# Expert outputs of a graph network's mixture layer: from VectorE multiply-adds to ScalarE scaling and TensorE sums in PSUM

## The chip, the cores and the metric

The kernel runs on one core of a Trainium2 chip. The metric is the device time of one execution in microseconds. The core has five engines with queues of their own: TensorE (PE in the rows; PEld its weight loads), VectorE (DVE), ScalarE (ACT), GpSimd (POOL) and SyncE (SP, which here only issues DMAs). They meet through semaphores.

## What is computed

Two layers on 32 graphs of 256 nodes with 128 features (8192 nodes, 64 tiles of 128). The first is a graph network (adjacency times features, two matrix products with RMS norm and SiLU). The second is a mixture of four experts whose gates come from graph attention over 524288 edges. Cut to what matters here:

```python
agg    = segment_softmax_sum(h[src], scores(src, dst), dst)     # graph attention, 4 heads x 4 experts
scores = layernorm(agg + b_gat).reshape(M, 4, 4).mean(heads)
topk_s, topk_i = top_k(scores, 2);  w = softmax(topk_s)
for e in range(4):
    g   = where(topk_i == e, w, 0).sum(-1)
    out = out + g[..., None] * (gelu(x @ W1[e] + b1[e]) @ W2[e] + b2[e])
return x + out
```

The expert outputs do not depend on the gates and are made long before them. What is late is the gates, and with them the last line's weighted sum of four expert outputs per node.

## The kernel before

The program is one launch with a hand-written order per engine. The stages, by the profile's time: sorting of the edges (to about 150 us), the graph network in a pipeline over 32 graphs (to about 460 us), the experts (to about 736 us), counting of edges (to about 905 us), and the **parts' stage**, from about 905 us to the end, which is all that the change touches.

The expert outputs (`eo`) of 64 tiles, 4 x 128 columns each, are ready when that stage begins. Those of the first 48 tiles lie in DRAM (`outputs`) in 12 blocks of 4 tiles; the last 16 tiles are kept in SBUF (`eo_kept`). GpSimd's 384 indirect gathers (L552), begun during the counting, fetch the table rows of the edges' sources, 96 per part. The stage does four **parts** g = 0 to 3 of 16 tiles each. A part is a chain over three engines:

- `hots_of` (L1400, VectorE) builds one-hot matrices; the copy of the gathered rows by heads (L948, ScalarE) is turned by TensorE (L782); `weights` (L1413, VectorE) does the softmax scans and ends in `back_ready`.
- TensorE turns the weights back (L787), ScalarE copies (L940), VectorE multiplies (`values`, L1437) and both split the rows into three bf16 pieces (`hi`, `remainder`, `mid`, `lowest`: L930, L1444, L935, L1449).
- TensorE sums them by owner in two batches of 48 matmuls (L795), into all eight PSUM banks: `sums[0]` is `ps_H`, `sums[1]` is `ps_four`, four banks each, four tiles of 3 x 24 columns to a bank. `take_bank` (L1451) reduces them; each raises `agg_out`.
- ScalarE issues a DMA that moves the odd half (L961); `merge` (L1461) waits for it; `gating` (L1501, about 40 small VectorE instructions) ends in `gates_ready`. In between, TensorE and ScalarE prepare the next part's marks (L771, L922 to L925).

**The weighted sum** stands between these steps. `combine(b)` (L1544, instruction L1557) is, for the block b of 4 tiles, 16 VectorE multiply-adds of 128 x 128 that read one expert's output, the gate column and the row of `xs`, and write `xs`. Part g does the four blocks of part g - 1: two while TensorE does the one-hot matmuls and two between `take_bank` and `merge`; the last part does two before `weights`, one and one. The blocks come back from DRAM through four SBUF slots (`SLOT_OF`, `load`, L453); a slot is free when its last block is combined, and SP stores each finished block (L485). After the last part's gates, VectorE does 8 kept tiles (32 multiply-adds), and the other 8 (`others`) go through ScalarE (scaling by the gates, L974) and GpSimd (three adds per tile, L590 to L594).

Of the kernel before, what the change touches and what calls it, by code (L numbers as in the profile page):

```python
# [24 lines left out]
GRAPHS, NODES, D = 32, 256, 128  # L25
# [39 lines left out]
PART_BLOCKS = BLOCKS // (PARTS - 1)  # L65
SLOT_OF = (0, 1, 0, 1, 0, 1, 2, 0, 1, 2, 3, 0)
KEPT_BLOCKS = 2

def build(nc, x, adj, eps, W1, b1, rms_w, W2, b2, W_gat, att_src, att_dst, b_gat, ln_g, ln_b,  # L70
# [4 lines left out]
    with ctx:  # L75
# [44 lines left out]
        def region(at):  # L120

            def take(shape, dt=fp32):
# [9 lines left out]
                if len(shape) > 1:  # L132
# [173 lines left out]
        sums = [ps_H[:, :, :, :].rearrange("p a b n -> p (a b n)").rearrange("p (g w) -> p g w", g=4), ps_four[:, :, :]]  # L306
# [17 lines left out]
                 "combined", "others_combined", "sum_chain", "gated", "iota_done", "zero_done"]  # L324
# [61 lines left out]

        def part_tiles(m, g):

            return m[:, g * PART_TILES:(g + 1) * PART_TILES]

        others = [(eo_kept[:, t, :], TILES - PAIR * KEPT + t) for t in range(KEPT_BLOCKS * BLOCK_TILES, PAIR * KEPT)]

# [3 lines left out]
        def _(sp):  # L396
# [100 lines left out]
            for b in range(KEPT_BLOCKS):  # L497
                sp.wait_ge(s["combined"], BLOCKS + b + 1)
                rstore(GROUPS - KEPT + BLOCK * b, BLOCK, out_stored[1])
            for b in range(KEPT // BLOCK - KEPT_BLOCKS):  # L500
                sp.wait_ge(s["others_combined"], BLOCK_TILES * (b + 1))
                rstore(GROUPS - KEPT + BLOCK * (KEPT_BLOCKS + b), BLOCK, out_stored[0])
            sp.wait_ge(out_stored[0], 16 * (KEPT // BLOCK - KEPT_BLOCKS))
            sp.wait_ge(out_stored[1], 16 * (BLOCKS + KEPT_BLOCKS))
# [5 lines left out]
        def _(pool):  # L510
# [73 lines left out]

            pool.wait_ge(s["gates_ready"], PARTS)
            for n, (of, t) in enumerate(others):
                row = xs[:, t, :]
                pool.wait_ge(s["gated"], n + 1)
                pool.tensor_tensor(of[:, 0:2 * D], of[:, 0:2 * D], of[:, 2 * D:4 * D], ALU.add).then_inc(s["sum_chain"], 1)  # L590
                pool.wait_ge(s["sum_chain"], 2 * n + 1)
                pool.tensor_tensor(of[:, 0:D], of[:, 0:D], of[:, D:2 * D], ALU.add).then_inc(s["sum_chain"], 1)
                pool.wait_ge(s["sum_chain"], 2 * n + 2)
                pool.tensor_tensor(row, row, of[:, 0:D], ALU.add).then_inc(s["others_combined"], 1)  # L594

        @block.tensor
        def _(pe):
# [178 lines left out]
            for g in range(PARTS):  # L776
                if g:
                    pe.wait_ge(s["agg_out"], 2 * g)
# [833 lines left out]
```

## Time and profile before

| | us |
|---|---|
| median of 3 runs (range) | 1173.28 (1170.89 to 1177.06) |
| profiled execution, whole time | 1177.35 |
| its span, first to last instruction | 1175.6 |
| parts' stage, from about 905 to the end of the span | about 270 |
| VectorE busy in the span | 918.5 (78%) |
| TensorE / ScalarE / GpSimd busy | 790.5 / 440.6 / 613.2 |

The profile is one execution. Times in its rows are from the start of the span. In a timeline row stand start, duration, engine, line, operation, output and inputs with their shape and the number of instructions merged (xN), and in brackets how long the engine had been idle and what released it.
### The profile page before, as it was taken

How to read it: one execution, taken by the hardware profiler on the slowest of the kernel's cores; microseconds unless marked ns; L12 is line 12 of the kernel's file. 1: busy time of each engine (PE TensorE's matmuls, PEld its weight loads, DVE VectorE, ACT ScalarE, POOL GpSimd, SP SyncE). 2: the span in 40 equal slices, each digit the busy share in tenths (PEclk: the TensorE clock that was granted, in tenths of full speed). 3: DMA queues.
4: the chain of work that ended last, by engine and by line, in shares of the span. 5: the costliest groups of instructions: out<-in, count | busy, mean ns of one | idle time of the engine just before them, and what ended most of it. 6: DMA issues, size and time to landing. Idle time of an engine off the chain costs nothing. (4 is left out here: it accounts for less than half of the span.)

```text
span 1175.6 us, 17882 instructions
## 1 busy us (share of the span) xinstructions
PE 790.5 (67%) x5180; PEld 677.8 (58%) x5180; DVE 918.5 (78%) x3070; ACT 440.6 (37%) x1069; POOL 613.2 (52%) x553
## 2 busy tenths in 40 slices
PE   0000089999999997987999999999997424131130
PEld 0000078887888885866888888888885314031030
DVE  7999967776888876999799800788887568888877
ACT  1009378775554553543555555000001212120203
POOL 2000000002777764057777777888888778888004
PEclk9999988997999996998999999655555555555555
DMA  7000011111222212121222221000000122616001
GB/s 248 0 0 1 7 42 38 44 43 45 48 53 56 56 9 12 54 78 46 64 81 81 63 63 10 7 7 7 7 6 9 10 48 51 182 29 203 19 22 36
DMA packets 73039, 55.42 MB, mean 47 GB/s; under 512 B 32534, under 2 KB 65689, under 8 KB 72988
## 3 DMA queue, kind: packets, MB, share of 16 engines
q1 hardware_dynamic: 56140, 48.72, 13.1%
q0 software_dynamic: 16384, 5.54, 5.7%
q10 hardware_dynamic: 464, 0.59, 0.2%
q8 instruction: 19, 0.31, 0.1%
q14 instruction: 32, 0.26, 0.1%
HBM read 36.65 MB, written 17.76 MB: 46 GB/s over the span
## 5 line engine op out<-in xcount | busy, mean ns | idle before, releaser
L552 POOL DMA_INDIRECT sb_arena<-table,sb_arena x384 | 465.1, 1211 | 169.7 <-issue 116.8
L536 POOL DMA_INDIRECT sb_late<-lists,sb_window_at x128 | 128.0, 1000 | 320.5 <-ACT sb_window_at L862 278.7
L727 PE MATMUL ps_four<-sb_late 128*128 128x64 bf16 x1232 | 160.3, 301 | 3.2 <-DVE sb_late L1287 0.9
L1285 DVE TENSOR_TENSOR sb_late<-sb_far_lo,sb_iota_lo 128x1792 bf16<-128x1792 bf16 x88 | 96.1, 1092 | 83.9 <-PE ps_four L727 81.7
L727 PEld LDWEIGHTS ps_four<-sb_late 128*128 128x128 bf16 x1232 | 141.9, 143 | 21.5 <-DVE sb_late L1287 19.6
L700 PE MATMUL ps_four<-sb_we,sb_arena 128*128 128x128 f32 x1024 | 131.9, 282 | 0.0
L700 PEld LDWEIGHTS ps_four<-sb_we,sb_arena 128*128 128x128 f32 x1024 | 119.7, 192 | 14.7 <-issue 14.7
L692 PE MATMUL ps_H<-sb_x2nT,sb_we 128*128 (+1 forms) x512 | 124.6, 388 | 0.0
L634 PE MATMUL ps_four<-sb_arena 128*128 128x256 f32 x128 | 38.8, 432 | 122.2 <-DVE sb_var L1145 122.2
L885 ACT ACTIVATE sb_arena<-ps_H,sb_be_c 128x256 f32<-128x256 f32 x256 | 107.2, 471 | 30.6 <-PE ps_H L692 28.7
L634 PEld LDWEIGHTS ps_four<-sb_arena 128*128 128x128 f32 x128 | 28.3, 227 | 129.4 <-DVE sb_arena L1198 122.5
L692 PEld LDWEIGHTS ps_H<-sb_x2nT,sb_we 128*128 128x128 f32 x512 | 95.1, 196 | 11.0
L818 ACT ACTIVATE sb_arena<-sb_arena,sb_owner_mid 128x368 f32<-128x368 f32 x128 | 76.8, 600 | 53.4 <-DVE sb_arena L1046 49.8
L626 PE MATMUL ps_H<-sb_arena,sb_w 128*128 128x256 f32 x256 | 78.5, 460 | 0.2 <-DVE sb_arena L1209 0.2
L1209 DVE SCALAR_TENSOR_TENSOR sb_arena<-ps_H,sb_b_c,sb_arena 128x256 f32<-128x256 f32 x128 | 53.1, 477 | 20.8 <-ACT sb_arena L844 19.6
L645 PE MATMUL ps_four<-sb_w,sb_arena 128*128 128x128 f32 x512 | 69.0, 290 | 0.0
L855 ACT ACTIVATE sb_arena<-sb_arena,sb_rms_c 128x256 f32<-128x256 f32 x128 | 54.6, 497 | 37.5 <-DVE sb_arena L1209 37.5
L669 PEld LDWEIGHTS ps_four<-sb_ones,sb_arena 128*128 128x128 f32 x512 | 60.8, 195 | 10.8 <-ACT sb_arena L834 10.8
L669 PE MATMUL ps_four<-sb_ones,sb_arena 128*128 128x1 f32 x512 | 60.7, 248 | 9.1 <-ACT sb_arena L839 9.1
L922 ACT ACT_TABLE_LOAD x1 | 1.3, 1283 | 170.6 <-PE ps_H L771 170.6
L645 PEld LDWEIGHTS ps_four<-sb_w,sb_arena 128*128 128x128 f32 x512 | 62.8, 200 | 3.9 <-issue 0.2
L782 PE MATMUL ps_H<-sb_ident,sb_iota_lo 128*128 128x128 f32 x24 | 7.1, 435 | 80.5 <-ACT sb_iota_lo L948 80.1
(244 smaller groups left out, 1466.4 us busy)
## 6 DMA issues: line engine op xcount, KB each, us to landing
outputs<-sb_arena SPq DMA_DIRECT2D x24, 512.0 KB
sb_arena<-outputs SPq DMA_DIRECT2D x12, 1024.0 KB, 6.7
sb_arena<-in_adj SPq DMA_DIRECT2D x32, 256.0 KB
sb_arena<-table,sb_arena POOLq DMA_INDIRECT x384, 2.9
sb_x2nT<-in_L_ffn_edge_index SPq DMA_DIRECT2D x8, 512.0 KB, 7.6
sb_xs<-in_x SPq DMA_DIRECT2D x32, 128.0 KB, 2.5
out_x<-sb_xs SPq DMA_DIRECT2D x16, 256.0 KB, 2.6
sb_late<-lists,sb_window_at POOLq DMA_INDIRECT x128
```

The source lines that it names most:

```text
L536: pool.indirect_dma_start(bk.bitcast(i32)[:, p * WINDOW:(p + 1) * WINDOW], None, lists, bass.IndirectOffsetOnAxis(ap=window_at[:, p:p + 1] ...
L552: pool.indirect_dma_start(rows[:, g, c, o, :], None, table[0:M, :], bass.IndirectOffsetOnAxis(ap=idxT[:, at:at + 1], axis=0), bounds_check ...
L626: last = nc.tensor.matmul(ps_H[:, q, c, :], w1[:, c * P:(c + 1) * P], aggT[:, q, :], start=True, stop=True)
L634: last = nc.tensor.matmul(ps_A, xn[:, p, mt, :], adjT[:, p, mt, :], start=(mt == 0), stop=(mt == 1))
L645: last = nc.tensor.matmul(ps_O[:, nt, :], ss[:, q, c, nt * P:(nt + 1) * P], w2[:, c, :], start=False, stop=(nt == 1 and c == HC - 1))
L669: last = nc.tensor.matmul(ps_Q[:, u:u + 1], sq[:, q, c, u * P:(u + 1) * P], ones[:, 0:1], start=(c == 0), stop=(c == HC - 1))
L692: last = nc.tensor.matmul(halfH[e][:, c * GROUP:(c + 1) * GROUP], we1[:, e, c * P:(c + 1) * P], x2nT[:, bass.ds(g * GROUP, GROUP)], start= ...
L700: last = nc.tensor.matmul(obank[k][:, (j // 2) * D:(j // 2 + 1) * D], hh[1 - p][:, j, k * P:(k + 1) * P], we2[:, j, :], start=False, stop= ...
L727: last = nc.tensor.matmul(ps_F, hot_lo[k][:, :, c], hot_hi[k][:, :, c], start=(first and c == 0), stop=(end and c == FB - 1))
L818: nc.scalar.activation(sign_out, owner, ACT.Sign, bias=owner_mid[:, o:o + 1], scale=2.0, accum_out=above[:, o:o + 1]).then_inc(s["above_co ...
L885: last = nc.scalar.activation(hh[p][:, 2 * e + c, :], halfH[e][:, c * GROUP:(c + 1) * GROUP], ACT.Gelu, bias=be1_c[:, 2 * e + c:2 * e + c ...
L1285: V.tensor_tensor(hot_lo[k], far_lo[:, bass.ds(b * FB, FB)].unsqueeze(1).to_broadcast([P, P, FB]), iota_lo[:, :, :], ALU.is_equal)
```

## The change

For the 12 blocks of the first three parts, VectorE's 16 multiply-adds per block are replaced by three steps on three engines: ScalarE scales the block's 16 pieces of 128 x 128 by their gates in place in the slot (`scale_block`), TensorE adds the four experts with four fp32 matmuls of 512 columns against the identity (`block_sum`), and VectorE adds the resulting bank to four tiles of `xs` in one instruction (`combine`). The banks for it come from packing six tiles instead of four to a bank in the one-hot sums (three banks per batch). Kept tiles: VectorE does ten, in groups of 4, 4 and 2; six go through ScalarE, TensorE (four experts and the row of `xs`) and ScalarE again; GpSimd's adds go. The stores of the kept tiles are of two tiles each.

```diff
+PER_BANK = 6
-KEPT_BLOCKS = 2
+KEPT_TILES = 10
...
+        sums = [ps_H[:, :, :, :].rearrange("p a b n -> p (a b n)").rearrange("p (g w) -> p g w", g=4)[:, 0:3, :], ps_four[:, 0:3, :]]
+        marks_bank = [halfH[2], bank_O[:, :]]
+        block_bank = [bank_S[:, :], halfH[3]]
...
+        def blocks_in(g):
+            if not g:
+                return [], []
+            of = [PART_BLOCKS * (g - 1) + b for b in range(PART_BLOCKS)]
+            return (of[:1], of[1:]) if g < PARTS - 1 else (of[:2], of[2:])
...
-            pool.wait_ge(s["gates_ready"], PARTS)
-            for n, (of, t) in enumerate(others):
...
             def mark(g):
                 if g:
-                    pe.wait_ge(s["agg_out"], 2 * g - 1)
+                    pe.wait_ge(s["agg_out"], 2 * g)
...
+            def block_sum(b):
+                pe.wait_ge(s["scaled"], b + 1)
+                some(pe, s["combined"], b - 1, None)
+                of = eo_back[SLOT_OF[b]]
+                for e in range(EXPERTS):
+                    last = nc.tensor.matmul(block_bank[b % 2], ident[:, :], of[:, :, e * D:(e + 1) * D],
+                                            start=(e == 0), stop=(e == EXPERTS - 1))
+                last.then_inc(s["block_in_psum"], 1)
...
                     last.then_inc(s["terms_in_psum"], 1)
+                for b in early:
+                    block_sum(b)
                 for k, ready in ((1, "back_ready"), (0, "exp_done")):
...
                 if g + 1 < PARTS:
                     mark(g + 1)
+                for b in late_:
+                    block_sum(b)
+            pe.wait_ge(s["agg_out"], 2 * PARTS)
+            for n, (of, t) in enumerate(others):
+                pe.wait_ge(s["gated"], n + 1)
+                for e in range(EXPERTS):
+                    nc.tensor.matmul(others_bank[n], ident[:, :], of[:, e * D:(e + 1) * D], start=(e == 0), stop=False)
+                nc.tensor.matmul(others_bank[n], ident[:, :], xs[:, t, :], start=False, stop=True).then_inc(s["others_in_psum"], 1)
...
+            def scale_block(b):
+                act.wait_ge(s["gates_ready"], b // PART_BLOCKS + 1)
+                act.wait_ge(eo_loaded[SLOT_OF[b]], 16 * turns(b))
+                for u in range(BLOCK_TILES):
+                    for e in range(EXPERTS):
+                        of = eo_back[SLOT_OF[b]][:, u, e * D:(e + 1) * D]
+                        last = nc.scalar.activation(of, of, ACT.Identity, scale=gates[:, b * BLOCK_TILES + u, e:e + 1])
+                last.then_inc(s["scaled"], 1)
...
+                if g < PARTS - 1:
+                    by_heads(g)
+                    for b in early:
+                        scale_block(b)
+                else:
+                    for b in early:
+                        scale_block(b)
+                    by_heads(g)
...
                 mid(2 * g + 1)
+                for b in late_[:2]:
+                    scale_block(b)
                 act.wait_ge(s["agg_out"], 2 * g + 2)
...
                 nc.scalar.activation(part_tiles(gates, g), part_tiles(sc, g), ACT.Exp).then_inc(s["gates_exp"], 1)
+                for b in late_[2:]:
+                    scale_block(b)
...
             def combine(b):
...
+                dve.wait_ge(s["block_in_psum"], b + 1)
+                to = xs[:, b * BLOCK_TILES:(b + 1) * BLOCK_TILES, :]
+                V.tensor_tensor(to, to, block_bank[b % 2].rearrange("p (t d) -> p t d", t=BLOCK_TILES), ALU.add).then_inc(s["combined"], 1)
...
                 take_bank(2 * g)
                 take_bank(2 * g + 1)
-                for b in before[len(before) // 2:]:
+                merge(g)
+                for b in late_[:1]:
                     combine(b)
-                merge(g)
                 gating(g)
-            for b in range(KEPT_BLOCKS):
-                combine(BLOCKS + b)
+                for b in late_[1:]:
+                    combine(b)
...
+            combine_kept(0, 4)
+            combine_kept(4, 4)
+            combine_kept(8, KEPT_TILES - 8)
```

So in the parts 1 and 2 one of the four blocks is early (`early`) and three are late (`late_`); in part 3 two and two. What is queued behind what is shown at two places. Line numbers in the rows of the change are those of the changed kernel.

VectorE from the end of part 2's gating to `weights` of part 3, before (L1541 ends the gating, L1404 is `hots_of`, L1557 the multiply-adds, L1418 the first instruction of `weights`):

```order
L1541 TENSOR_TENSOR sb_gates<-sb_gates,sb_gs 128x64
L1404 TENSOR_TENSOR sb_arena<-sb_arena,sb_w 128x1024 x6
L1557 SCALAR_TENSOR_TENSOR sb_xs<-sb_arena,sb_gates,sb_xs 128x128 x32
L1418 TENSOR_TENSOR sb_arena<-ps_H,sb_arena 128x384
L1420 TENSOR_TENSOR sb_arena<-ps_H,sb_arena 128x384
```

The same place in the change (L1605 ends the gating, L1612 is `combine`, L1467 `hots_of`, L1481 the first of `weights`):

```order
L1605 TENSOR_TENSOR sb_gates<-sb_gates,sb_gs 128x64
L1612 TENSOR_TENSOR sb_xs<-sb_xs,ps_four 128x512
L1612 TENSOR_TENSOR sb_xs<-sb_xs,ps_H 128x512
L1467 TENSOR_TENSOR sb_arena<-sb_arena,sb_w 128x1024 x6
L1612 TENSOR_TENSOR sb_xs<-sb_xs,ps_four 128x512
L1612 TENSOR_TENSOR sb_xs<-sb_xs,ps_H 128x512
L1481 TENSOR_TENSOR sb_arena<-ps_H,sb_arena 128x384
```

Blocks 6 and 7 now stand ahead of the one-hots, and 8 and 9 between these and `weights`; each is one instruction that waits for a bank.

ScalarE over the same stretch, before (L968 is the gates' exponential, L948 the copy by heads, L951 the softmax's exponential):

```order
L968 ACTIVATE sb_gates<-sb_sc 128x64
L948 ACTIVATE sb_iota_lo<-sb_arena 128x384 x2
L951 ACTIVATE sb_arena<-sb_arena 128x384
L940 ACTIVATE sb_arena<-ps_four 128x3x4x32 x2
L930 ACTIVATE sb_late<-sb_arena 128x48x24 x2
```

ScalarE there in the change (L1015, L981 and L996 are those three, L973 is `scale_block`):

```order
L1015 ACTIVATE sb_gates<-sb_sc 128x64
L973 ACTIVATE sb_arena<-sb_arena,sb_gates 128x128 x48
L981 ACTIVATE sb_iota_lo<-sb_arena 128x384 x2
L996 ACTIVATE sb_arena<-sb_arena 128x384
L963 ACTIVATE sb_arena<-ps_four 128x3x4x32 x2
```

The scaling of three blocks (7, 8 and 9), 48 instructions, now stands between the gates and the copy by heads.

TensorE in the change, from part 2's one-hot sums to those of part 3 (L809; L772 are the marks, L781 `block_sum`, L794 and L801 the two turns, which before followed each other directly as L782 and L787):

```order
L809 MATMUL ps_four<-sb_late,sb_arena 64x72 x48
L772 MATMUL ps_H<-sb_arena,sb_epsI 128x384
L772 MATMUL ps_four<-sb_arena,sb_epsI 128x384
L781 MATMUL ps_H<-sb_arena,sb_ident 128x512 x4
L781 MATMUL ps_four<-sb_arena,sb_ident 128x512 x4
L781 MATMUL ps_H<-sb_arena,sb_ident 128x512 x4
L794 MATMUL ps_H<-sb_ident,sb_iota_lo 128x128 x6
L781 MATMUL ps_four<-sb_arena,sb_ident 128x512 x4
L781 MATMUL ps_H<-sb_arena,sb_ident 128x512 x4
L801 MATMUL ps_four<-sb_ident,sb_arena 128x128 x6
```

The sums of the blocks 5, 6 and 7 stand ahead of the first turn, and those of 8 and 9 behind it.

## Rows read from the trace of the kernel before

**Rows 1.** The page: span, and the granted TensorE clock in 40 slices.
```profile
span 1175.6 us, 17882 instructions
...
PEclk9999988997999996998999999655555555555555
```

**Rows 2.** Timeline, part 1's last take_bank to weights of part 2.
```profile
999.55 1.41 DVE L1458 TENSOR_REDUCE sb_late<-ps_four 64x192 f32<-64x576 f32 x2 [0.89 <-PE ps_four L795]
...
1000.89 4.27 DVE L1557 SCALAR_TENSOR_TENSOR sb_xs<-sb_arena,sb_gates,sb_xs 128x128 f32<-128x128 f32 x16
...
1006.62 4.29 DVE L1557 SCALAR_TENSOR_TENSOR sb_xs<-sb_arena,sb_gates,sb_xs 128x128 f32<-128x128 f32 x16 [1.46 <-DMA sb_arena<-outputs]
...
1010.82 0.22 DVE L1467 TENSOR_TENSOR sb_a_dst<-sb_late,sb_far_e 128x64 f32<-128x64 f32 x1
...
1027.38 0.22 DVE L1541 TENSOR_TENSOR sb_gates<-sb_gates,sb_gs 128x64 f32<-128x64 f32 x1
1027.64 3.70 DVE L1404 TENSOR_TENSOR sb_arena<-sb_arena,sb_w 128x1024 bf16<-128x1024 bf16 x6
...
1031.26 0.55 DVE L1418 TENSOR_TENSOR sb_arena<-ps_H,sb_arena 128x384 f32<-128x384 f32 x1
```

**Rows 3.** Timeline, part 0: merge with no multiply-adds ahead of it, then gating.
```profile
949.30 0.23 DVE L1467 TENSOR_TENSOR sb_a_dst<-sb_late,sb_far_e 128x64 f32<-128x64 f32 x1 [4.87 <-DMA sb_late<-sb_late]
...
953.41 0.19 DVE L1505 TENSOR_SCALAR sb_late<-sb_late 128x64 f32<-128x64 f32 x1
...
964.77 0.26 ACT L968 ACTIVATE sb_gates<-sb_sc 128x64 f32<-128x64 f32 x1 [14.41 <-DVE sb_sc L1536]
...
965.86 0.22 DVE L1541 TENSOR_TENSOR sb_gates<-sb_gates,sb_gs 128x64 f32<-128x64 f32 x1
```

**Rows 4.** Timeline, part 2's last take_bank to weights of part 3.
```profile
1061.07 1.41 DVE L1458 TENSOR_REDUCE sb_late<-ps_four 64x192 f32<-64x576 f32 x2 [0.88 <-PE ps_four L795]
...
1063.95 7.94 POOL L552 DMA_INDIRECT sb_arena<-table,sb_arena  x1 [0.31 <-issue]
...
1091.23 8.48 DVE L1557 SCALAR_TENSOR_TENSOR sb_xs<-sb_arena,sb_gates,sb_xs 128x128 f32<-128x128 f32 x32
1092.69 2.21 ACT L948 ACTIVATE sb_iota_lo<-sb_arena 128x384 f32<-128x384 f32 x2 [6.16 <-DMA sb_arena<-table,sb_arena]
...
1093.99 1.86 PE L782 MATMUL ps_H<-sb_ident,sb_iota_lo 128*128 128x128 f32 x6 [30.10 <-ACT sb_iota_lo L948]
...
1099.63 0.55 DVE L1418 TENSOR_TENSOR sb_arena<-ps_H,sb_arena 128x384 f32<-128x384 f32 x1
```

**Rows 5.** Timeline, part 3's last take_bank to the end of the multiply-adds.
```profile
1129.44 1.41 DVE L1458 TENSOR_REDUCE sb_late<-ps_four 64x192 f32<-64x576 f32 x2 [4.35 <-PE ps_four L795]
1130.78 4.27 DVE L1557 SCALAR_TENSOR_TENSOR sb_xs<-sb_arena,sb_gates,sb_xs 128x128 f32<-128x128 f32 x16
...
1151.57 9.46 ACT L974 ACTIVATE sb_x2nT<-sb_x2nT,sb_gates 128x128 f32<-128x128 f32 x32 [1.09 <-DVE sb_gates L1541]
1151.58 16.54 DVE L1557 SCALAR_TENSOR_TENSOR sb_xs<-sb_x2nT,sb_gates,sb_xs 128x128 f32<-128x128 f32 x32
```

**Rows 6.** Timeline of TensorE: fp32 passes of 256, 128 and 384 columns.
```profile
725.60 2.05 PE L700 MATMUL ps_four<-sb_we,sb_arena 128*128 128x128 f32 x16
727.49 1.89 PE L692 MATMUL ps_H<-sb_x2nT,sb_we 128*128 x8
...
942.91 2.93 PE L771 MATMUL ps_H<-sb_arena,sb_epsI 128*128 128x384 f32 x4
```

**Rows 7.** Windows (PE, PEld, DVE, ACT, POOL busy; clock; DMA): experts' start, and counting.
```profile
462.00:464.00 2.00, 2.00 (x6) 1.55 (x6) 0.13 (x2) 0.28 (x1) 0.00 (x0) 0.50 0.11 16
...
466.00:468.00 2.00, 2.00 (x11) 1.74 (x11) 1.93 (x4) 1.99 (x6) 0.00 (x0) 1.00 1.39 39
...
750.00:800.00 50.00, 48.14 (x378) 43.16 (x377) 43.88 (x55) 0.00 (x0) 41.77 (x28) 0.50 0.07 7
```

**Rows 8.** The page's DMA issues: size and time to landing.
```profile
sb_arena<-outputs SPq DMA_DIRECT2D x12, 1024.0 KB, 6.7
```

More of the change, by code:

```diff
@@ L583, in _ @@
                     edge_tile(2 * j + 1, 1)
-            pool.wait_ge(s["gates_ready"], PARTS)
-            for n, (of, t) in enumerate(others):
[L588 to L594, printed above, removed]
         @block.tensor
@@ L975, in _, with keep_sum @@
                 last.then_inc(s["gated"], 1)
+            def keep_sum(n):
+                act.wait_ge(s["others_in_psum"], n + 1)
+                nc.scalar.activation(xs[:, others[n][1], :], others_bank[n], ACT.Identity).then_inc(s["others_combined"], 1)
+            gate(0)
+            gate(1)
+            for n in range(2, len(others)):
+                gate(n)
+                keep_sum(n - 2)
+            keep_sum(len(others) - 2)
+            keep_sum(len(others) - 1)
         @block.vector
@@ L1453, in take_bank @@
                 dve.wait_ge(s["agg_in_psum"], k + 1)
[L1454 to L1458 removed]
+                for first, past, each in ((0, 2, PER_BANK), (2, 3, BATCH - 2 * PER_BANK)):
+                    by_bank = sums[k % 2][0:OWN, first:past, 0:each * 3 * ROW].rearrange("p g (t u s v) -> p g t u s v", u=2, s=3, v=ROW)
+                    at = BATCH // 2 * (k % 2) + first * PER_BANK // 2
+                    for u, m in enumerate((agg, odd)):
+                        o = m[k // 2 % 2][0:OWN, at:at + (past - first) * each // 2, :].rearrange("p (g t) v -> p g t v", g=past - first)
+                        last = V.reduce_sum(o, by_bank[:, :, :, u, :, :].rearrange("p g t s v -> p g t v s"), AX.X)
                 last.then_inc(s["agg_out"], 1)
@@ L1567, in _ @@
                 if g == PARTS - 1:
-                    combine(before.pop(0))
-                    combine(before.pop(0))
+                    for b in early:
+                        combine(b)
                 weights(g)
@@ L1575, in _, with combine_kept @@
                 lowest(2 * g + 1)
-                for b in before[:len(before) // 2]:
-                    combine(b)
+                if g < PARTS - 1:
+                    for b in early:
+                        combine(b)
                 take_bank(2 * g)
                 take_bank(2 * g + 1)
-                for b in before[len(before) // 2:]:
+                merge(g)
+                for b in late_[:1]:
                     combine(b)
-                merge(g)
                 gating(g)
-            for b in range(KEPT_BLOCKS):
-                combine(BLOCKS + b)
+                for b in late_[1:]:
+                    combine(b)
+            def combine_kept(first, n):
+                base = (EXPERTS - 1) * first
+                for e in range(EXPERTS):
+                    for u in range(n):
+                        row = xs[:, TILES - PAIR * KEPT + first + u, :]
+                        if e:
+                            dve.wait_ge(s["comb_chain"], base + (e - 1) * n + u + 1)
+                        last = V.scalar_tensor_tensor(row, eo_kept[:, first + u, e * D:(e + 1) * D],
+                                                      gates[:, TILES - PAIR * KEPT + first + u, e:e + 1], row, ALU.mult, ALU.add)
+                        if e < EXPERTS - 1:
+                            last.then_inc(s["comb_chain"], 1)
+                        elif u % PAIR:
+                            last.then_inc(s["combined"], 1)
+            combine_kept(0, 4)
+            combine_kept(4, 4)
+            combine_kept(8, KEPT_TILES - 8)
 _INS = ["x", "adj", "L0_gnn_epsilon", "L0_gnn_W1", "L0_gnn_b1", "L0_gnn_rms_weight", "L0_gnn_W2", "L0_gnn_b2",
```

69 lines of the change are left out of this document (27 added, 42 removed).

## The prediction, blind

> **What bounds the kernel now.** I read the page first, then the timelines of the three places where one part hands over to the next, and last the windows that show TensorE's clock. The page [rows 1] says that the span is 1175.6 us and that in its last 14 slices the granted clock is about half. Everything that the change touches lies in the last 270 us, so the prediction is a sum over a few boundaries there; the rest stays as it is.
>
> I write W(g) for the start of `weights` of part g. Two readings from the rows decide what a saved VectorE microsecond is worth.
>
> First, from W(2) at 1031.26 [rows 2] to the end of part 2's second `take_bank` at 1062.48 [rows 4] it is 31.2 us, and from W(3) at 1099.63 [rows 4] to 1130.85 [rows 5] it is 31.2 us again. By the kernel's order two blocks of multiply-adds stand inside the first stretch and one inside the second. A block is 4.27 us [rows 2], and yet the stretches are equal: TensorE's one-hot sums cover them. Taking multiply-adds out **there** is worth nothing.
>
> Second, between `take_bank` and `merge` they are seen: part 1 goes from 1000.96 to 1010.82 [rows 2] with two blocks and a wait of 1.46 for a load. But part 0 [rows 3], with no block there, has VectorE idle for 4.87 at the same place, for the DMA of the odd half. So about half of what is taken out here comes back as that wait.
>
> The next readings give the length of each boundary before. `take_bank` of part 1 to W(2): 1000.96 to 1031.26, 30.3 us [rows 2]. `take_bank` of part 2 to W(3): 1062.48 to 1099.63, 37.2 us [rows 4]; here the gathers are late too (the copy by heads waits 6.16 for them, until 1092.69), and the 8.48 of two blocks end last. `take_bank` of part 3 to the gates: 1130.85 to 1151.57, 20.7 us; then 16.54 of multiply-adds on the kept tiles [rows 5].
>
> **The change part by part: the price of a block.** ScalarE scales 16 pieces of 128 x 128. The same instruction on the kept tiles takes 9.46 for 32 [rows 5], 0.296 each: 4.7 us per block. VectorE's add of 512 columns from PSUM has no row; the nearest is 0.55 for 384 columns from PSUM [rows 2], so about 0.7.
>
> TensorE's four fp32 matmuls of 512 columns are eight passes. No row of before has such a block. From both sides: four passes of 384 columns at a clock of 0.50 take 2.93 [rows 6], so eight of 512 take 2.93 x 2 x 512/384 = **7.8**; eight passes of 256 columns at 1.00 take 1.89 [rows 6], so eight of 512 take **3.8**. Which clock is granted? In the counting stage TensorE is busy 48.14 of 50 us and has 0.50 throughout, with narrow bf16 matmuls; when the experts begin, with fp32 passes of 256 columns back to back, the window from 462 has 0.50 and that from 466 has 1.00 [rows 7]. The sums are like the second. I take the middle, **5.8**, for a block that comes after a pause and 3.8 for one directly behind another.
>
> The Trainium skill says it the same way for the second case and not for the first: its page "TensorE: Matmul & The Clock Gate" (Part 1, the HAM clock gate) has the throttled clock as the default, which sustained activity releases. By that rule the sums end at the high clock and the total below is about +17; by the row of the counting stage, where a busy engine was not released, it would be about +35. The experts' windows are why I lean to the first.
>
> **From `take_bank` of part 1 to W(2).** In the change: the wait for the odd half, 4.9; `merge`, 949.30 to 953.41, 4.1; block 1's add, 0.7 (its sum is ready after the marks' 2.9 and 5.8, that is at 8.7, when VectorE comes at 9.0); gating, 953.41 to 966.08, 12.7 [all rows 3]. That is 22.4 to the gates. Then block 3. ScalarE has it behind the gates' exponential, which ends 1.05 before the gates are done (965.03 against 966.08 [rows 3]). From there 4.7 to scale, 5.8 to sum, 0.7 to add: 10.2 after the gates. The one-hots (3.7 [rows 2]) are queued behind that add on VectorE, so W(2) comes at 22.4 + 10.2 + 3.7 = 36.3, against 30.3: **+6.0**.
>
> **From `take_bank` of part 2 to W(3).** Again 22.4 to the gates. ScalarE now has 48 scalings (blocks 7, 8, 9) ahead of the copy by heads, where before the copy was next. On the path: 14.2 for these, from 1.05 ahead of the gates; the copy, 2.2; TensorE's turn, which ends at 1095.85, 0.95 after the copy [rows 4]; only then the sums of 8 and 9, since TensorE has them behind the turn, 5.8 + 3.8; then block 9's add, 0.7, because VectorE has it ahead of `weights`. Together 26.6 after the gates; the adds of 6 and 7 and the one-hots lie inside it (10.2 + 3.7). W(3) comes at 49.0, against 37.2: **+11.8**. The gathers, last here before, end sooner: while VectorE does blocks, a GpSimd gather that comes next is stretched (7.94 [rows 4]), and these blocks go. It gives nothing, since the copy stands behind the scalings.
>
> **Part 3 and the end.** To the gates 22.4 instead of 20.7: **+1.7** (4.9 of waiting for 4.27 of multiply-adds, plus block 10's add). Then VectorE has block 11's add and 40 multiply-adds. Before, 32 took 16.54 beside GpSimd's adds, but 16 took 4.27 without them [rows 5], 0.267 each: 0.7 + 10.7 = 11.4. TensorE has 60 passes of 128 columns: from 16 in 2.05 [rows 6] 7.7, or by the low price (2.93/4 x 128/384 = 0.244) 14.7; with ScalarE's first tile (1.2) and last copy (0.3) the second branch ends at 9.2 to 16.2. Middle 12.7: **-3.8**, with -5.1 and -0.3 as ends.
>
> **Small terms.** `take_bank` has four reductions for two on the same columns: 0 to 0.4 each (0.19 is a small instruction [rows 3]), four times: +0.8. On ScalarE the odd half's DMA is queued behind the scaling of blocks 1 and 2; block 2's load (6.7 [rows 8]) can be issued only after block 0's add, so its scaling ends about with the sums: +0.5. Block 0's sum ahead of the second turn: 0, or 2.0 at the low price.
>
> **Sum**: 6.0 + 11.8 + 1.7 - 3.8 + 0.8 + 0.5 = **+17.0 us**. Against the profiled execution's 1177.35 that is 1194.4. That execution lies 4.1 above the median of the runs shown, so the median should come to 1173.28 + 17.0 = 1190.3, about **1190**.
>
> **The rivals.** *All sums at the high clock*: block 3 saves 2.0, block 8 saves 2.0, the end 1.3, the small terms fall away (1.3): +10.4, 1184. For it speaks 466 onward [rows 7]; against it, that every burst starts after a pause. *All at the low clock*: block 3 +2.0 and block 1 late by 1.7; blocks 8 and 9 +6.0 and block 5 late by 1.7; the end +3.5, block 0 +2.0, small +0.8: +34.7, 1208. For it speaks the counting stage, against it the experts' start.
>
> *Faster*: VectorE is the only thing that counts, and ScalarE and TensorE always have the sum ready when it asks. Then W(2) comes at 22.4 + 1.4 + 3.7 = 27.5 (-2.8), W(3) at 22.4 + 1.4 + 3.7 + 1.4 = 28.9 (-8.3; the gathers ended 30.2 after `take_bank` before, but a good 6.9 of that was stretched), part 3 +1.7, the end -5.1, small +0.8: -13.7, 1160. It decides where a block needs no more than 1.7 from the gates' exponential to its add. The rows give 4.7 + 5.8 + 0.7 = 11.2, and 4.7 is ScalarE's own price, in a row of the same instruction. Against it, then.
>
> *No change*: the waits cost only what the end gives back. W(3) would have to come 8 us sooner than reckoned, which would need the copy by heads ahead of the scalings; the order has it behind.
>
> **How the numbers follow.** The sum as reckoned has 0.72, all high 0.12, all low 0.08, faster 0.04, no change 0.04. The range 1181 to 1204 takes in the forecast with its prices and the high clock, and leaves out the two last cases and most of the low clock. About 0.5%, 5.9 us, is what a measurement of this kernel can tell from no change: faster by more 0.04, within 0.04, slower by more 0.92.
>
> **What would show it.** Right: VectorE idle ahead of the one-hots of part 2 for some 9 us and ahead of `weights` of part 3 for some 12, in both cases released by TensorE's sums; the copy by heads of part 3 behind 48 scalings, no longer released by a gather; stretches of 31 us inside the parts as before; clock 1.00 in the sums behind 1.2 GHz starts; multiply-adds at the end at 0.27. Wrong: sums of a block under 3 us, scalings under 0.2 each, or W(3) less than 40 us after `take_bank`.

## The result, and the profile after

| | before | change |
|---|---|---|
| median of 6 runs (range), us | 1173.83 (1170.64 to 1177.06) | 1181.38 (1179.3 to 1182.34) |
| profiled execution, us | 1177.35 | 1180.44 |
| its span | 1175.6 | 1178.7 |
| W(0) to the end of the span | 263.0 | 267.1 |

The change is slower: ratio 1.0063, interval 1.0040 to 1.0086, which is 4.7 to 10.1 us (7.55 between the medians). The prediction said +17.0, with 1181 at the very edge of its range. The last row of the table is the cleanest measure in what follows: W(0) is the start of `weights` in part 0, and all that the change touches comes after it. W(0) itself comes between 907.0 and 915.8 us in the 13 profiles of this study, whatever the kernel, so single spans are compared from W(0) on. By that measure the change costs 4.1 us.

The page of the change, first its span and TensorE's granted clock, to be held against [rows 1]:

```profile
span 1178.7 us, 18234 instructions
...
PEclk9999989888999996998999999555555555666757
```

The last slices were all 5; now five of the last six are 6 or 7. The higher clock comes with the blocks' sums: of the two halves of the change that are run alone below, blocks_only ends in 757765 on this line and tail_only, without those sums, in 555556.

The timeline of the change from part 1's last `take_bank` to W(2), against [rows 2] (L1522 `take_bank`, L1531 the start of `merge`, L1013 its exponential on ScalarE, L1535 what waits for that, L973 `scale_block`, L781 `block_sum`, L1612 `combine`):

```profile
998.55 1.54 DVE L1522 TENSOR_REDUCE sb_late<-ps_four 64x144 f32<-64x432 f32 x4 [4.22 <-PE ps_four L809]
...
1002.64 0.23 DVE L1531 TENSOR_TENSOR sb_a_dst<-sb_late,sb_far_e 128x64 f32<-128x64 f32 x1 [2.54 <-DMA sb_late<-sb_late]
...
1002.87 3.98 PE L781 MATMUL ps_H<-sb_arena,sb_ident 128*128 128x512 f32 x8
...
1005.16 0.23 DVE L1535 TENSOR_TENSOR sb_late<-sb_late 128x64 f32<-128x64 f32 x1 [1.90 <-ACT sb_far_e L1013]
...
1006.69 3.60 PE L781 MATMUL ps_four<-sb_arena,sb_ident 128*128 128x512 f32 x8
...
1020.33 4.76 ACT L973 ACTIVATE sb_arena<-sb_arena,sb_gates 128x128 f32<-128x128 f32 x16
...
1025.14 6.56 PE L781 MATMUL ps_H<-sb_arena,sb_ident 128*128 128x512 f32 x8 [14.86 <-ACT sb_arena L973]
...
1031.75 0.69 DVE L1612 TENSOR_TENSOR sb_xs<-sb_xs,ps_H 128x512 f32<-128x512 f32 x1 [9.54 <-PE ps_H L781]
1032.35 3.72 DVE L1467 TENSOR_TENSOR sb_arena<-sb_arena,sb_w 128x1024 bf16<-128x1024 bf16 x6
...
1036.00 0.55 DVE L1481 TENSOR_TENSOR sb_arena<-ps_H,sb_arena 128x384 f32<-128x384 f32 x1
```

VectorE waits 9.54 us for block 3's sum, with the one-hots behind it. That is the chain as forecast: 4.76 to scale, 6.56 to sum, 0.69 to add. Two things differ: the odd half is waited for 2.54 us, not 4.9, and L1535 waits another 1.90 for ScalarE, so that `merge` to the gates takes 18.8 instead of 17.5. That this boundary comes out at +5.6, near the forecast's +6.0, is in part luck: the shorter wait, the longer `merge` and the longer sum cancel.

From part 2's last `take_bank` to W(3), against [rows 4] (L981 is the copy by heads):

```profile
1069.51 0.23 DVE L1531 TENSOR_TENSOR sb_a_dst<-sb_late,sb_far_e 128x64 f32<-128x64 f32 x1 [2.15 <-DMA sb_late<-sb_late]
...
1087.36 14.11 ACT L973 ACTIVATE sb_arena<-sb_arena,sb_gates 128x128 f32<-128x128 f32 x48
...
1101.37 2.19 ACT L981 ACTIVATE sb_iota_lo<-sb_arena 128x384 f32<-128x384 f32 x2
1102.65 1.86 PE L794 MATMUL ps_H<-sb_ident,sb_iota_lo 128*128 128x128 f32 x6 [5.00 <-ACT sb_iota_lo L981]
1104.31 4.46 PE L781 MATMUL ps_four<-sb_arena,sb_ident 128*128 128x512 f32 x8
1108.61 3.60 PE L781 MATMUL ps_H<-sb_arena,sb_ident 128*128 128x512 f32 x8
1108.81 0.69 DVE L1612 TENSOR_TENSOR sb_xs<-sb_xs,ps_four 128x512 f32<-128x512 f32 x1 [6.81 <-PE ps_four L781]
1112.24 0.69 DVE L1612 TENSOR_TENSOR sb_xs<-sb_xs,ps_H 128x512 f32<-128x512 f32 x1 [2.75 <-PE ps_H L781]
1112.85 0.55 DVE L1481 TENSOR_TENSOR sb_arena<-ps_H,sb_arena 128x384 f32<-128x384 f32 x1
```

The copy by heads, which before waited for a gather, stands behind 48 scalings; the sums of 8 and 9 come after it; `weights` comes last. This is the second chain of the prediction, link for link.

The end, against [rows 5] (L1647 the kept tiles on VectorE, L1030 the last copy on ScalarE):

```profile
1164.17 10.58 DVE L1647 SCALAR_TENSOR_TENSOR sb_xs<-sb_x2nT,sb_gates,sb_xs 128x128 f32<-128x128 f32 x40
...
1174.78 0.28 ACT L1030 ACTIVATE sb_xs<-ps_H 128x128 f32<-128x128 f32 x1 [0.84 <-PE ps_H L823]
```

Here 40 multiply-adds take 10.58 us, 0.265 each; before, 32 took 16.54, 0.517 each, beside GpSimd's adds. And the end has a second half that the timeline of working engines does not show: the queues' own instructions of the program's exit. GpSimd's last operation and the exit's rows (queue and instruction, count, shortest/median/longest ns, start), before:

```profile
1166.99 0.45 POOL L594 TENSOR_TENSOR sb_xs<-sb_xs,sb_x2nT 128x128 f32<-128x128 f32 x1
...
L75 POOLq DRAIN  x1: 8424/8424/8424, 1167.0 to 1167.0; - x1
L75 SPq DRAIN  x1: 7/7/7, 1172.5 to 1172.5; - x1
```

and in the change:

```profile
1065.52 1.00 POOL L564 DMA_INDIRECT sb_arena<-table,sb_arena  x1 [0.30 <-issue]
...
L76 POOLq DRAIN  x1: 23501/23501/23501, 1050.9 to 1050.9; - x1
L76 SPq DRAIN  x1: 7/7/7, 1178.5 to 1178.5; - x1
```

Before, GpSimd's queue ends in a drain that begins with its last add and takes 8.4 us, to 1175.4; the span ends at 1175.6. SP, with all stores landed, was through at 1172.5. In the change GpSimd has nothing to do at the end; its drain starts at 1050.9, while the gathers still run (to 1066.5), is over at 1074.4, and SP's stores end the program. From the last operation to the end of the span it is 7.5 us before (1168.1 to 1175.6) and 3.6 after (1175.1 to 1178.7). Of these 3.8 us the drain accounts for 2.9, from SP's 1172.5 (and the 0.2 by which SP's drain lies ahead of the end of the span in the change) to 1175.6; the other 0.9 is that SP is through 4.4 us after the last operation before and 3.4 after it in the change.

Stretch by stretch (all ends and starts are those of the rows above or their like in the other parts):

| stretch | before | change | measured | forecast |
|---|---|---|---|---|
| `weights` to `take_bank`, four parts | 125.5 | 126.6 | +1.1 | +1.3 |
| part 0: `take_bank` to W(1) | 25.3 | 24.6 | -0.7 | 0 |
| part 1: `take_bank` to W(2) | 30.3 | 35.9 | +5.6 | +6.0 |
| part 2: `take_bank` to W(3) | 37.2 | 45.5 | +8.4 | +11.8 |
| part 3: `take_bank` to the gates | 20.7 | 19.3 | -1.4 | +1.7 |
| gates to the last operation | 16.6 | 11.5 | -5.1 | -3.8 |
| last operation to the end of the span | 7.5 | 3.6 | -3.8 | 0 |
| sum from W(0) on | 263.0 | 267.1 | **+4.1** | **+17.0** |

### The profile page after: what moved, and what is told of

It is laid out like the page before. It is cut to its first block and busy times, and to the rows that moved or that the text cites. A ratio compares the mean times of both kernels' runs of the same rounds, so it can differ in the third digit from the quotient of the medians.

```text
span 1178.7 us, 18234 instructions
## 1 busy us (share of the span) xinstructions
PE 850.9 (72%) x5336; PEld 710.6 (60%) x5336; DVE 870.6 (74%) x2914; ACT 495.4 (42%) x1259; POOL 576.5 (49%) x529
## 5 line engine op out<-in xcount | busy, mean ns | idle before, releaser
L564 POOL DMA_INDIRECT sb_arena<-table,sb_arena x384 | 441.5, 1150 | 169.3 <-issue 116.8
L728 PE MATMUL ps_four<-sb_late 128*128 128x64 bf16 x1232 | 157.1, 301 | 6.4 <-DVE sb_late L1350 2.1
L908 ACT ACTIVATE sb_arena<-ps_H,sb_be_c 128x256 f32<-128x256 f32 x256 | 106.9, 472 | 30.5 <-PE ps_H L693 28.9
L627 PEld LDWEIGHTS ps_H<-sb_arena,sb_w 128*128 128x128 f32 x256 | 57.6, 236 | 9.8 <-issue 0.5
```

Of the source, the lines that this page charges most:

```text
L564: pool.indirect_dma_start(rows[:, g, c, o, :], None, table[0:M, :], bass.IndirectOffsetOnAxis(ap=idxT[:, at:at + 1], axis=0), bounds_check ...
L627: last = nc.tensor.matmul(ps_H[:, q, c, :], w1[:, c * P:(c + 1) * P], aggT[:, q, :], start=True, stop=True)
L728: last = nc.tensor.matmul(ps_F, hot_lo[k][:, :, c], hot_hi[k][:, :, c], start=(first and c == 0), stop=(end and c == FB - 1))
L908: last = nc.scalar.activation(hh[p][:, 2 * e + c, :], halfH[e][:, c * GROUP:(c + 1) * GROUP], ACT.Gelu, bias=be1_c[:, 2 * e + c:2 * e + c ...
```

## The experiments

The first theory, A, is that of the prediction: what costs time is the order in ScalarE's queue and the sums on TensorE behind it, and each chain can be cut where a step stands behind another without need. The rival B is that these steps cost what they cost wherever they stand. Eleven kernels ran, 4 to 10 times each; times are medians, ratios are against runs of the kernel before on the same chip, and "from W(0)" is that of the profiled execution (before: 263.0).

| kernel | us | ratio (interval) | from W(0) |
|---|---|---|---|
| gate_first | 1174.62 | 1.0000 (0.9974 to 1.0026) | 262.6 |
| heads_first | 1169.92 | 0.9959 (0.9937 to 0.9982) | 256.2 |
| both | 1157.50 | 0.9840 (0.9784 to 0.9896) | 242.7 |
| tail_only | 1165.66 | 0.9915 (0.9888 to 0.9941) | 252.4 |
| blocks_only | 1191.89 | 1.0147 (1.0105 to 1.0189) | 276.6 |
| drain_back | 1169.40 | 0.9968 (0.9944 to 0.9991) | 257.1 |
| load_late | 1180.60 | 1.0061 (1.0036 to 1.0085) | 266.2 |
| third_slot | 1153.66 | 0.9843 (0.9806 to 0.9880) | 242.7 |
| exp_first | 1175.10 | 0.9992 (0.9968 to 1.0015) | 262.5 |
| slots_apart | 1151.79 | 0.9791 (0.9755 to 0.9826) | 237.3 |
| all_moves | 1146.21 | 0.9747 (0.9715 to 0.9779) | 234.2 |

### The two queue orders: gate_first, heads_first, both

gate_first, on the change:

```diff
+                for b in late_[2:]:
+                    scale_block(b)
                 act.wait_ge(s["gates_e"], g + 1)
                 nc.scalar.activation(part_tiles(gates, g), part_tiles(sc, g), ACT.Exp).then_inc(s["gates_exp"], 1)
-                for b in late_[2:]:
-                    scale_block(b)
```

> The change with one move: ScalarE scales the third late block (blocks 3 and 7) ahead of its wait for the gates' exponential instead of behind it. Theory A (the loss is ScalarE's queue order: scalings stand between the gates and what the next part needs): from take_bank of part 1 to weights of part 2 35.9 us becomes about 31 (block 3's load lands only just before, so its sum is still waited for), from take_bank of part 2 to weights of part 3 45.5 becomes about 41, no other stretch moves; the whole about 1172. Rival B (the loss is TensorE's price of the sums, 3.6 to 6.7 us a block on the path): the sums come at another time at the same price, both stretches move by less than 2 us each; 1178 to 1182.

Part 1's boundary fell from 35.9 to 30.1 as expected. Part 2's stayed, at 45.3, and there the expectation missed. ScalarE in gate_first, part 2:

```profile
1081.87 4.78 ACT L973 ACTIVATE sb_arena<-sb_arena,sb_gates 128x128 f32<-128x128 f32 x16 [1.09 <-DVE sb_gates L1605]
...
1088.65 4.78 ACT L973 ACTIVATE sb_arena<-sb_arena,sb_gates 128x128 f32<-128x128 f32 x16 [2.00 <-DMA sb_arena<-outputs]
```

Block 7 had gone ahead, but 8 waits for the gates themselves, 9 then 2.00 for its load, and the sum of 8, behind the turn, takes 5.59 instead of 4.46:

```profile
1094.62 1.86 PE L794 MATMUL ps_H<-sb_ident,sb_iota_lo 128*128 128x128 f32 x6 [19.38 <-ACT sb_iota_lo L981]
1096.28 5.59 PE L781 MATMUL ps_four<-sb_arena,sb_ident 128*128 128x512 f32 x8
```

TensorE had stood idle for 19.38 us ahead of the turn instead of 5.00, and the granted clock over that sum is 0.50 up to 1098.0 and 0.67 from there to 1101.5; in the change it is 0.61 up to 1106.5 and 1.00 behind that. So one of the two chains was cut, and the time, 1174.6, stayed above the 1172 that A gave.

heads_first, on the change (TensorE's and VectorE's order follow it):

```diff
-                if g < PARTS - 1:
-                    by_heads(g)
-                    for b in early:
-                        scale_block(b)
-                else:
-                    for b in early:
-                        scale_block(b)
-                    by_heads(g)
+                by_heads(g)
+                for b in early:
+                    scale_block(b)
```

> The change with part 3 alone reordered: the copy by heads ahead of the scaling of blocks 8 and 9, the sum of 9 behind the second turn on TensorE, and VectorE's adds of 8 and 9 behind the splitting into pieces instead of ahead of weights. Theory A: block 7 (scaled behind the gates) now ends last, so from take_bank of part 2 to weights of part 3 45.5 us becomes about 35, the stretch inside part 3 stays at 31 to 32; the whole about 1171. Rival B: the two sums only move into the stretch inside part 3, which grows by about what the boundary loses (8 us or more); 1178 to 1182.

Part 2's boundary (L983 the copy by heads, L1609 `combine`):

```profile
1091.92 2.19 ACT L983 ACTIVATE sb_iota_lo<-sb_arena 128x384 f32<-128x384 f32 x2
...
1097.60 0.69 DVE L1609 TENSOR_TENSOR sb_xs<-sb_xs,ps_H 128x512 f32<-128x512 f32 x1 [8.48 <-PE ps_H L781]
```

It is 34.6 instead of 45.5. The copy by heads stands straight behind block 7's scaling, and what VectorE waits for is now block 7's sum. The stretch inside part 3 stays at 31.35, so the sums of 8 and 9 did not only move, as B had it.

both is the two edits together, with one block early in every part.

> The change with both moves, and part 3 ordered like the parts 1 and 2 (one early block, three late, the third scaled ahead of the gates' exponential). The same arithmetic is done by the same engines at the same prices. Theory A: take_bank of part 1 to weights of part 2 about 31 (block 3's load still late), of part 2 to weights of part 3 about 26 to 27; the whole about 1157 to 1160, which is faster than the kernel before by 1.2 to 1.4%. Rival B: not below 1173, since 12 sums of 3.6 to 6.7 us have to be paid somewhere on the path.

Boundaries of 30.5 and 26.0, and 24 us less than the change. The same scalings, sums and adds are all still there: B falls. The work is cheap where it stands beside other work, and it cost what it did by its place in the queue.

### The last part alone, and the blocks alone

tail_only is the kernel before with the change's kept tiles (ten on VectorE, six through ScalarE and TensorE, stores of two tiles) and its blocks as they were; blocks_only is the opposite.

> The kernel before with the change's last part alone: VectorE ten kept tiles, ScalarE and TensorE six, no adds on GpSimd, stores of two tiles. The blocks of the first three parts are done by VectorE as before. Theory A: from the gates to the last operation 16.5 us becomes about 11.5 and the stores behind it shorten too; 5 to 9 us faster than before, 1165 to 1169. Rival (the end is bound by the stores or by the end of the program, not by the operations): less than 2 us faster, 1172 to 1174.

> The change's blocks of parts 1 to 3, but the last part as before: VectorE 8 kept tiles, ScalarE and GpSimd 8. Theory A (the boundary terms were near right and the term of the end was the one mis-sized): W(2) about 36 us after take_bank and W(3) about 45.5 after it, as in the change; after the gates 17.2 us to the last operation, then again some 7.5 to the end of the span, since GpSimd's queue ends in a drain of about 8.4 us behind its last add, as before. Time 1186 to 1191, 13 to 17 us above the kernel before. Theory B (the boundaries cost less than the trace of the change shows, and the last part gave little): 1179 to 1183, like the change.

From W(0), tail_only is 10.5 us shorter than before and blocks_only 13.6 longer; their sum, +3.1, is near the change's +4.1. In the medians it is -9.8 and +18.6, with wide intervals, and +7.6 for the change. So the last part gives some 10 us (9.4 of the 10.5 lie behind the gates), where the prediction had 3.8, and from W(0) the blocks cost less than the 20.8 that its other terms add up to; the medians alone, 12 to 22 us by the interval, would not exclude 20.8. The median of blocks_only, 1191.9, lies 0.9 above the expected range. The boundaries in blocks_only are those of the change (35.95 and 45.47), and its end has the drain again:

```profile
L76 POOLq DRAIN  x1: 8424/8424/8424, 1182.9 to 1182.9; - x1
L76 SPq DRAIN  x1: 7/7/7, 1188.9 to 1188.9; - x1
```

### Is it the drain? drain_back

To tail_only, one GpSimd instruction is added:

```diff
+            pool.wait_ge(s["others_combined"], len(others))
+            spare = others[-1][0]
+            pool.tensor_tensor(spare[:, 0:D], spare[:, 0:D], spare[:, D:2 * D], ALU.add)
```

> tail_only (the kernel before with the change's last part), and one GpSimd add of 128 x 128 on a spent tile, behind the last of the six tiles. The output is the same. Theory A (GpSimd's drain behind work at the end sets the end of the program): the add ends about 1 us after the last copy, a drain of about 8 us follows it and ends last; the stretch from the last kept tile to the end of the span goes from 3.6 back to 8 or 9, the time rises by 4 to 5 us over tail_only, to about 1170. Theory B (the late stores of 256 KB made the difference): the drain is short or hidden by the stores, time as tail_only, 1165 to 1166.

The add and the exit's rows:

```profile
1161.15 0.81 POOL L591 TENSOR_TENSOR sb_x2nT<-sb_x2nT 128x128 f32<-128x128 f32 x1 [76.56 <-ACT sb_xs L985]
```

```profile
L75 POOLq DRAIN  x1: 8774/8774/8774, 1161.1 to 1161.1; - x1
L75 SPq DRAIN  x1: 7/7/7, 1165.3 to 1165.3; - x1
```

SP is through at 1165.3, and the span goes on to 1170.1 for GpSimd. A single add of 0.81 us brings a drain as long as eight tiles' adds did, and the time rises by 4.7 us from W(0) on (3.7 between the medians, which are from two chips). So the drain is shown to cost what it lasts beyond SP. The smaller stores are no more than a small part of the gain: SP is through 3.7 to 3.8 us after VectorE's last operation with stores of two tiles (the change, tail_only, drain_back) and 4.4 with stores of four (before, blocks_only).

The end of the drain follows one measure in all 13 profiles: it comes 7.9 to 8.0 us after GpSimd's last operation, whether that is an add (before 1167.4 to 1175.4) or an indirect gather (the change 1066.5 to 1074.4).

### The wait for the odd half: load_late, exp_first

load_late, on the change: SP issues block 1's load only after part 0's odd half has moved.

```diff
                 if k:
                     sp.wait_ge(s["agg_in_psum"], 2 * k)
+                if b == 1:
+                    sp.wait_ge(odd_moved[0], 16)
```

> The change, with the load of block 1 waiting for part 0's odd-half DMA. Theory A (the 4.87 of rows 3, from which the prediction took its wait, held a load of 1 MB in flight at the same time): merge of part 0 waits about 2.2 us for the odd half instead of 4.1, the same as in the parts 1 to 3; everything after comes about 2 us sooner: 1179 to 1180 against 1181.4. Theory B (part 0's wait has another cause): the wait stays at 4.1 and the time at 1181.

Part 0 in the change, SP's load of 1 MB, the odd half's DMA and the wait:

```profile
941.99 0.39 SPq L472 DMA_DIRECT2D sb_arena<-outputs  x1
...
943.57 0.53 ACTq L1008 DMA_DIRECT2D sb_late<-sb_late  x1
...
947.63 0.23 DVE L1531 TENSOR_TENSOR sb_a_dst<-sb_late,sb_far_e 128x64 f32<-128x64 f32 x1 [4.10 <-DMA sb_late<-sb_late]
```

and in load_late, with the load behind (L1015 is `merge`'s second exponential on ScalarE):

```profile
947.09 0.53 ACTq L1010 DMA_DIRECT2D sb_late<-sb_late  x1
...
949.36 0.23 DVE L1533 TENSOR_TENSOR sb_a_dst<-sb_late,sb_far_e 128x64 f32<-128x64 f32 x1 [2.30 <-DMA sb_late<-sb_late]
949.42 0.39 SPq L474 DMA_DIRECT2D sb_arena<-outputs  x1
...
951.67 0.28 ACT L1014 ACTIVATE sb_late<-sb_late 128x64 f32<-128x64 f32 x1
951.82 0.28 ACT L1015 ACTIVATE sb_far_e<-sb_far_e 128x64 f32<-128x64 f32 x1
952.12 0.23 DVE L1537 TENSOR_TENSOR sb_late<-sb_late 128x64 f32<-128x64 f32 x1 [2.15 <-ACT sb_far_e L1015]
```

The cause of the long wait is shown: 4.10 becomes 2.30 without the load beside it, and in the four kernels below that keep this edit it is 2.2 to 2.3 as well. The time stays, though (1180.6; part 0's boundary 24.55 against 24.64). A new wait of 2.15 took its place: ScalarE has the next part's marks ahead of `merge`'s exponentials, and the marks wait for both of TensorE's batches. exp_first turns that round:

```diff
-                if g + 1 < PARTS:
-                    mark(g + 1)
                 act.wait_ge(s["merge_in"], g + 1)
...
+                if g + 1 < PARTS:
+                    mark(g + 1)
```

> load_late, and ScalarE does merge's two exponentials ahead of the next part's marks. In load_late the wait for the odd half fell as expected, and merge to gates rose from 16.8 to 18.6, so that part 0 came no sooner. Theory A (ScalarE's marks, which now wait for both batches of take_bank, are the next wait behind the odd half): merge to gates is 16.8 to 17.5 in the parts 0 to 2, about 1.8 us less in each; all together 5 to 6 us: 1175 to 1176. Theory B (merge's own work is longer, or the marks' delay turns up ahead of the next weights): merge to gates as in load_late, or the gain returns; 1180.

`merge` to gates fell from 18.6, 18.8 and 18.5 in the parts 0 to 2 to 16.8, 17.6 and 17.2; 0.7 of it came back ahead of W(3). From W(0) that is 3.7 us less than in load_late, 262.5, about the kernel before's 263.0; between the medians, from two chips, it is 5.5. So the wait is the one that A named, and its gain of 5 to 6 us is borne out by the medians and not by the profiles.

### The rest of the boundary: third_slot, slots_apart, all_moves

In both, block 3 still waits: its slot is free only when block 1 is added. third_slot, on both:

```diff
-SLOT_OF = (0, 1, 0, 1, 0, 1, 2, 0, 1, 2, 3, 0)
+SLOT_OF = (0, 1, 0, 2, 0, 1, 2, 0, 1, 2, 3, 0)
...
+                if b in (1, 3):
+                    sp.wait_ge(odd_moved[b // 2], 16)
...
-                        and SLOT_OF[loaded] <= b // PART_BLOCKS + 1:
+                        and (SLOT_OF[loaded] <= b // PART_BLOCKS + 1 or loaded == 3):
```

> The kernel both (exponential of the gates and copy by heads ahead of the scalings, one block early in every part), with block 3 in the third slot, so that its load needs not wait for block 1's add, and the loads of blocks 1 and 3 behind the odd half's DMA. Theory A: gates to W(2) falls from 9.1 to about 5 us, since block 3 is scaled and summed before the gates are done; part 0's wait for the odd half falls from 4.1 to 2.2. Together 5 to 6 us: 1151 to 1153. Theory B (TensorE's sums of blocks 1 to 3 in a row, not the load, end last): gates to W(2) stays at 8 to 9, and only the 2 us come: 1155 to 1156.

The gates to W(2) fell from 9.1 to 4.85, as A said, and nothing was gained: 242.7 from W(0), as in both, and a ratio of 0.9843 against 0.9840. Part 2's stretch from `weights` to `take_bank` rose from 32.4 to 36.8. Its rows (L975 `scale_block`, L783 `block_sum`, L803 the second turn):

```profile
1023.17 4.79 ACT L975 ACTIVATE sb_arena<-sb_arena,sb_gates 128x128 f32<-128x128 f32 x16 [6.27 <-DMA sb_arena<-outputs]
...
1028.01 6.44 PE L783 MATMUL ps_four<-sb_arena,sb_ident 128*128 128x512 f32 x8 [10.15 <-ACT sb_arena L975]
1034.28 0.82 PE L803 MATMUL ps_four<-sb_ident,sb_arena 128*128 128x128 f32 x6
```

Block 4's load is issued only after block 2's add, which stands behind the gating; with W(2) earlier, its scaling and sum are now what the second turn waits for. slots_apart gives block 4 the slot that block 1 leaves:

```diff
-SLOT_OF = (0, 1, 0, 2, 0, 1, 2, 0, 1, 2, 3, 0)
+SLOT_OF = (0, 1, 0, 2, 1, 0, 2, 1, 0, 2, 3, 1)
```

> third_slot, with block 4 in the slot that block 1 frees between take_bank and merge (blocks 5, 7, 8 and 11 moved with it). In third_slot the gates to W(2) fell to 4.85 as expected, and part 2's stretch from weights to take_bank rose from 31 to 36.8. Theory A (block 4's load waits for block 2's add, which stands behind the gating, and its sum then holds the second turn up): the load is issued some 13 us sooner, part 2's stretch is 31 again, and 5 to 6 us are gained: 1148. Theory B (the sum of the early block itself delays the turn): the stretch stays above 34; 1152 or more.

```profile
1025.65 4.77 ACT L975 ACTIVATE sb_arena<-sb_arena,sb_gates 128x128 f32<-128x128 f32 x16
```

The scaling waits for no load any more, part 2's stretch is 31.0, and 5.4 us are gained from W(0), the gain that A gave; the median stays 4 above its figure.

all_moves is slots_apart with exp_first's order.

> slots_apart with exp_first's order on ScalarE. If both theories A hold and the gains add: 1148 less 5 to 6, 1142 to 1143. If the gates then come before the sums of the late blocks are done, half of the second gain goes: 1145.

1146.2, 2.5% under the kernel before (interval 2.2 to 2.9%): the fastest kernel here, though 1 us above the worse case of the expectation. From W(0) the second step gave 3.1 us: 2.0 and 1.4 at the boundaries of the parts 0 and 1, and nothing in part 2, where VectorE comes earlier and now waits for block 5's sum instead:

```profile
1059.66 0.69 DVE L1609 TENSOR_TENSOR sb_xs<-sb_xs,ps_H 128x512 f32<-128x512 f32 x1 [1.28 <-PE ps_H L783]
```

## Why the prediction was right in its chains and wrong in its sum

**The chains were right.** Both waits that the prediction put on the path are there, where it put them and released by what it said: 9.54 us ahead of the one-hots of part 2 (some 9 forecast) and 6.81 and 2.75 ahead of `weights` of part 3 (some 12). heads_first, gate_first and both show by intervention that the queue order is the cause. The stretches inside the parts stayed at 31 to 32. "Faster", by which the sums are always ready, is excluded by these rows; what both, and still more slots_apart, show is that another order makes it nearly true.

**The prices of the blocks were near.** Scaling 4.76 against 4.7; the add 0.69 against 0.7. Sums: after a pause 6.56 (block 3) against 5.8, directly behind another 3.60 against 3.8, and 4.46 for block 8, which comes behind the turn, where 5.8 was taken. The windows of TensorE in the change (PE, PEld, DVE, ACT, POOL busy; clock; DMA) show both levels within block 3's sum and the one behind:

```profile
1022.00:1028.00 6.00, 2.86 (x4) 1.31 (x5) 0.20 (x1) 5.18 (x13) 4.78 (x5) 0.50 0.78 226
1028.00:1031.70 3.70, 3.70 (x8) 1.51 (x7) 0.00 (x0) 2.82 (x10) 2.79 (x4) 0.60 0.12 14
1033.70:1037.40 3.70, 3.68 (x8) 1.44 (x8) 3.67 (x7) 0.00 (x0) 3.09 (x3) 1.00 0.89 233
```

It begins at 1.2 GHz, after 14.86 us of idle, and the next has 2.4. The low-clock rival, +34.7, falls: the longest sum of a block in the change is 6.68 us, not 7.8. The high-clock rival, +10.4, is the nearest in number, but by luck: its mechanism falls with block 3's 6.56, and what brought the time down were the odd half and the end.

The Trainium skill's page "TensorE: Matmul & The Clock Gate" (Part 1: The HAM clock gate) says that activity releases a throttled default. These rows agree with that; the counting stage [rows 7], busy 48.14 of 50 us at 0.50, does not.

**The first step that failed is "the wait for the odd half, 4.9".** It was taken from [rows 3], the only place before where it showed, and reasoned as "about half of what is taken out here comes back as that wait". It measured 2.54, 2.15 and 2.14 in the parts 1 to 3: 7.9 us less over three boundaries. The row was true, but not for those parts: SP issues a load of 1 MB 1.5 us ahead of the odd half's DMA in part 0 (before at 943.01 and 944.46, in the change at 941.99 and 943.57), no load is in flight there in the parts 1 to 3, and load_late shows that this load makes the difference. A part of it, 1.35 and 1.5 in the parts 1 and 2, came back as the wait behind ScalarE's marks. The diff shows that `mark` now waits for both batches; the prediction counted its time on TensorE, and not that ScalarE's marks then stand ahead of `merge`'s exponentials. exp_first shows that this is a term. What is left of +11.8 against +8.4 is block 8's sum (1.3 less) and small parts.

**The other failed step is the end, "-3.8, with -5.1 and -0.3 as ends".** From the gates to the last operation it measured -5.1, which is one of its ends: 0.265 for a multiply-add without GpSimd was right, and the branch over TensorE's 60 passes ended 0.3 us behind VectorE's. But the term stopped at the last operation, and put what follows at nothing. There 3.8 us more were gained: 2.9 by which GpSimd's drain had outlasted SP, and 0.9 by which SP is through sooner. The page and the timeline do not count such instructions as busy, and the prediction did not look for them. drain_back shows the drain's cost by itself. Together 5.1 us were missed at the end (8.9 gained, 3.8 forecast).

**The sum**: 17.0, less 4.5 at the boundaries of the parts 0 to 2 and 3.1 in part 3 (odd half, marks, block 8), less 5.1 at the end and 0.2 of small terms, is the 4.1 of the profile. Why the medians stand 7.6 apart and the profiles 4.1 from W(0) is not settled; W(0) itself varies by more than that, and the part of the change's cost that lies in this difference stays open.

## What to carry to other kernels

A wait that a change will uncover is priced by its row only if the row's surroundings will be the same: look at what else, a large transfer above all, was in flight when the row was taken. When an engine's last work is removed, read the program's exit too, since a queue's drain can outlast the stores: here it ended some 8 us after GpSimd's last operation, and cost nothing as soon as that lay well ahead of the end. And when work is spread over three engines, give the order in each queue as much thought as the prices: here the same instructions were 0.6% slower or 2.5% faster by their places, and each wait removed uncovered the next until that was moved as well.

## What the hardware showed that was not expected

GpSimd's queue ended in a drain that was over 7.9 to 8.0 us after GpSimd's last operation in every profile, and no program ended before its drain. With adds last, its row is 8.4 us long (before, blocks_only) or 8.8 (drain_back, a single add of 128 x 128). With the gathers last, the row is 22.5 to 23.5 us long, but it begins while gathers still run; it was over long before the stores and cost nothing.

A VectorE multiply-add of 128 x 128 took 0.517 us on average beside GpSimd's adds and 0.265 without. The row of before [rows 5] shows that it is GpSimd and not ScalarE: its first five multiply-adds follow each other at 0.26 us while ScalarE already scales; GpSimd's first add starts at 1153.01, from 1152.89 on the other 27 take 0.56 each, and they stay at about 0.53 from 1161.1 on, when ScalarE is done. The gathers do not do this to the multiply-adds, 16 of which take 4.27 beside them [rows 2]; there it is the gather that is stretched, to 7.94 us beside two blocks [rows 4], where the gathers between `take_bank` and `merge` take 1.00 each in the change, which has no multiply-adds there. The Trainium skill's page "SBUF — State Buffer" (Who interferes with whom) has VectorE and GpSimd share one pair of ports under an exclusive lock. These rows agree with that, and no run here shows the lock itself.

The DMA of the odd half, SBUF to SBUF, was waited for 2.1 to 2.7 us with no load in flight and 4.0 to 4.9 with a load of 1 MB issued 1.5 us ahead of it.
